# A deformable convolution's offset convolution with its three kernel rows side by side in TensorE's array, and rows and taps that nobody reads left out

## What is computed

```python
om = _conv2d(x, w_off, b_off, STRIDE, PAD)      # 27 channels: off_y, off_x, m for each of 9 taps
off_y, off_x, m = jnp.split(om, 3, axis=1)
mask = jax.nn.sigmoid(m)
py = base_y + kgy + off_y; px = base_x + kgx + off_x
...
sampled = corner(y0, x0, ...) + corner(y0, x0 + 1, ...) + corner(y0 + 1, x0, ...) + corner(y0 + 1, x0 + 1, ...)
out = jnp.einsum('bckhw,ock->bohw', sampled * mask[:, None], weight) + bias
...
x = x + _L0_conv_ref(_gn(x), ...)               # deformable convolution, group norm
x = x + _L1_conv_ref(_gn(x), ...)               # two 3x3 convolutions with ternary weights, batch norms, relu
```

## Time and profile before

| | |
|---|---|
| median of 3 runs | 311.93 us (311.05 to 311.96) |
| profiled execution, its own time | 310.99 us |
| its span | 309.2 us |
| PE matmul busy | 273.2 us (88%) |
| PE weight load busy | 239.6 us (77%) |
| DVE busy | 206.3 us (67%) |
| ACT busy | 177.0 us (57%) |
| POOL busy | 133.6 us (43%) |
| mean granted TensorE clock | 0.978 |

### The profile page before, as it was taken

One profiled execution on the slowest core, in us unless ns is written; L12 is line 12 of the kernel. 1 busy time (PEld: TensorE's weight loads), 2 busy tenths in 40 slices (PEclk: granted clock), 3 DMA queues, 4 the chain that ended last, 5 costly groups with the idle time before them and its releaser, 6 DMA issues.

```text
span 309.2 us, 5008 instructions
## 1 busy us (share of the span) xinstructions
PE 273.2 (88%) x1712; PEld 239.6 (77%) x1712; DVE 206.3 (67%) x426; ACT 177.0 (57%) x334; POOL 133.6 (43%) x189
## 2 busy tenths in 40 slices
PE   2999999799999989998998989998899976999900
PEld 2768787699989889997998889997777755777700
DVE  3798666688998899759878788785253625006184
ACT  2549654688866968977789777882043006321052
POOL 8350376376666858777657966503000000000031
PEclk9999999999999999999999999999999997999985
DMA  7900966844333332333323333200000000000006
GB/s 248 330 3 3 302 202 183 271 126 136 116 114 106 113 88 77 103 107 108 108 64 106 104 103 111 83 0 2 0 0 2 0 0 0 0 2 0 2 36 243
DMA packets 25031, 28.60 MB, mean 93 GB/s; under 512 B 2461, under 2 KB 22541, under 8 KB 25000
## 3 DMA queue, kind: packets, MB, share of 16 engines
q1 hardware_dynamic: 24496, 26.98, 27.2%
q10 hardware_dynamic: 504, 1.24, 1.2%
HBM read 19.87 MB, written 6.78 MB: 86 GB/s over the span
## 4 chain that ended last, share of the span: by engine, by line
PE 71%; DVE 16%; ACT 8%; issue 2%; DMA 1%; ACTq 0%
PE PS L683 23%; PE PS L571 10%; PE PS L534 9%; PE PS L607 5%; PE PS L589 4%; PE PS L608 4%; PE PS L609 4%; PE PS L591 4%; PE PS L590 4%; DVE slo L1179 3%; DVE st L1081 2%; ACT vhi L847 2%; DVE vlo L1186 2%; ACT shi L840 2%; DVE xb L1279 2%
## 5 line engine op out<-in xcount | busy, mean ns | idle before, releaser
L453 POOL TENSOR_TENSOR vt<-rowm,hat 128x1026 f32<-128x1026 f32 x36 | 70.8, 1968 | 37.5 <-PE PS L571 36.8
L1179 DVE TENSOR_TENSOR slo<-PS,shi 114x512 fp32r<-114x512 f32 x72 | 53.6, 751 | 12.8 <-ACT shi L840 12.6
L1186 DVE TENSOR_TENSOR vlo<-PS,vhi 128x576 fp32r<-128x576 f32 (+2 forms) x84 | 50.3, 619 | 13.0 <-ACT vhi L847 13.0
L840 ACT ACTIVATE shi<-PS 114x512 fp32r<-114x512 f32 x72 | 46.3, 652 | 20.0 <-PE PS L571 19.7
L571 PE MATMUL PS<-ident,vt 128*114 128x128 f32 x324 | 47.4, 275 | 1.4 <-DVE nsm L1032 0.7
L847 ACT ACTIVATE vhi<-PS 128x576 fp32r<-128x576 f32 (+2 forms) x84 | 44.0, 546 | 7.4 <-PE PS L591 5.1
L589 PE MATMUL PS<-shi,patch 114*128 114x288 f32 x136 | 43.8, 322 | 1.9 <-DVE omh L1329 1.5
L607 PE MATMUL PS<-vhi,wdhi 128*128 128x256 f32 x144 | 43.0, 299 | 2.1 <-ACT xb L854 2.0
L683 PE MATMUL PS<-xhi,q 128*128 128x512 f32 x144 | 39.6, 422 | 4.2 <-ACT xhi L915 4.2
L473 POOL TENSOR_TENSOR xb<-xb,xs 128x512 f32<-128x512 f32 x3 | 3.7, 1274 | 87.3 <-ACT xb L920 87.3
L591 PE MATMUL PS<-shi,patch 114*128 114x288 f32 x136 | 40.8, 300 | 0.0
(11 more groups left out here) (146 smaller groups left out, 438.4 us busy)
## 6 DMA issues: line engine op xcount, KB each, us to landing
patch<-xt SPq DMA_DIRECT2D x136, 114.0 KB
xt<-xtt SPq DMA_DIRECT2D x4, 1024.0 KB, 7.1
xs<-in_x SPq DMA_DIRECT2D x3, 512.0 KB, 7.4
out<-xb SPq DMA_DIRECT2D x6, 256.0 KB, 2.3
wraw<-in_L_conv_w SPq DMA_DIRECT2D x2, 576.0 KB, 9.0
omr<-omr SPq DMA_DIRECT2D x8, 128.0 KB, 4.2
wd_raw<-in_L_conv_weight ACTq DMA_DIRECT2D x1, 576.0 KB, 6.5
xs<-in_x SPq DMA_DIRECT2D x2, 256.0 KB, 4.2
```

The source lines that it names most:

```text
L453: g.tensor_tensor(vt[:, n % 2, :, :].rearrange("p t (r j) -> p t r j", r=WR), rowm[:, n % 2, :, :].unsqueeze(3).to_broadcast([P, TAPS, WR, ...
L840: a.activation(shi[:, n % 2, lo:hi], S_PS[:, lo:hi], ACT.Copy).then_inc(shi_ok, 1)
L1179: d.tensor_tensor(slo[:, n % 2, lo:hi], S_PS[:, lo:hi], shi[:, n % 2, lo:hi], ALU.subtract).then_inc(slo_ok, 1)
L1186: last = d.tensor_tensor(places(vlo), src, places(vhi), ALU.subtract)
```

## The change

**Offset convolution.** The weights of the three kernel rows stand side by side: `woffT` is now 96 columns (three groups of 32) for each of three horizontal taps, in a `hi` and a `lo` copy. One matmul applies a whole kernel row's column to the centre rows: 6 matmuls on `xhi` (hi and lo weights) and 3 on `xlo` for a half image, 9 instead of 18. The product of `xlo` with the weights' `lo` part is left out. The result, 96 partitions of 512 pixels for each half, goes with the bias through ACT (`tail`) to `omc`, a buffer of 34 rows. Its three groups have still to be shifted by a row against each other and added: PE transposes 32 partitions x 128 pixels at a time (`turn_offsets`, 24 transposes an image, three steps of 8; each step waits until the one before has landed), and DVE adds the three with one reduction a half image (`offsets`). That leaves the offsets at 128 positions (four rows) at once; `replicate` now makes the shifted copies by four DMAs of fewer bytes, `masks` works on 128 partitions x 72 elements instead of 32 x 288, and `largest` likewise.

**Order.** In the head `turn_offsets(b)` is put between the halves of later images; `xlo` of image 1 is made by POOL between its two sums of weights instead of by DVE; SP stores image 0's pixels ahead of `replicate(0)`, and image 1's only after `fetch_patches(0)`; ACT's and DVE's calls are rearranged.

**Left out.** The first pair of an image (rows -1, 0) takes only taps 3 to 8 and the last pair (rows 31, 32) only taps 0 to 5: 192 columns instead of 288. For the ninth chunk the transposes of `vt` are six of 64 columns instead of nine of 128. In the ternary convolutions, taps that would read a border row of zeros do 15 rows instead of 16.

```diff
+        omr = sb("omr", [P, B, K + 1, CH, GRP])
...
-            woffT = sb("woffT", [P, TAPS, P], F32R, own)
+            woffT = sb("woffT", [P, 2, K, STACK], F32R, own)
...
+        def taps_at(n, u):
+            s = 4 * (n % CH) + 2 * u
+            return (K, TAPS) if s == 0 else (0, 2 * K) if s == H else (0, TAPS)
+        def weights_at(m, n, part):
+            v = m.rearrange("k (t p) -> k t p", p=P)
+            t0, t1 = PARTS[part]
+            return v[:, t0:t1, :] if pairs(n) == 2 else v[:, t0:min(t1, 2 * K), 0:P // 2]
...
+        TAP_ORDER = [[K + 1] + [k for k in range(TAPS) if k != K + 1], [k for k in range(TAPS) if k != K + 1] + [K + 1]]
+        def tap_rows(h, k):
+            return (1 if (h, k // K) == (0, 0) else 0), H // 2 - (1 if (h, k // K) == (1, K - 1) else 0)
...
             def replicate(b):
-                sp.wait_ge(off_t, 2 * b + 2)
                 sp.wait_ge(mask_ok, b + 1)
-                for q in range(1, 4):
...
+                for ky in range(1, K):
+                    for src, dst, j in ((0, ky * GRP, 0), (P - ky * GRP, 0, 1)):
+                        n = P - ky * GRP if j == 0 else ky * GRP
+                        sp.dma_start(omr[dst:dst + n, b, K - 1 - ky, j:j + H // 4, :],
+                                     omr[src:src + n, b, K - 1, 0:H // 4, :]).then_inc(rep_in[b], 16)
...
+                if i == 0:
+                    pool.wait_ge(xn_ok, 2)
+                    g.tensor_tensor(inner(xlo, 1), square(plain(1)), inner(xhi, 1), ALU.subtract).then_inc(xlo_second, 1)
...
-                for k in range(TAPS):
-                    r = b % RING * ROWS + h * (H // 2) + k // K
-                    last = t.matmul(OFF_PS[(2 * b + h) % 4], woffT[:, k, :], (xhi, xlo)[part][:, r:r + H // 2, k % K:k % K + W],
-                                    start=(k == 0 and part == 0), stop=(k == TAPS - 1 and part == 1))
+                r = b % RING * ROWS + 1 + h * (H // 2)
+                for kx, lo in PASSES[part]:
+                    last = t.matmul(OFF_PS[(2 * b + h) % 4], woffT[:, lo, kx, :], (xhi, xlo)[part][:, r:r + H // 2, kx:kx + W],
+                                    start=(part, lo, kx) == (0, 0, 0), stop=(part, kx) == (1, K - 1))
...
+            PASSES = [[(kx, lo) for lo in range(2) for kx in range(K)], [(kx, 0) for kx in range(K)]]
+            def turn_offsets(b):
+                if b == 0:
+                    pe.wait_ge(pads, 11)
+                pe.wait_ge(off_tail, 2 * b + 2)
+                for step in range(K):
+                    if step:
+                        pe.wait_ge(off_t, 2 * (K * b + step))
+                    for j in range(4):
+                        for half in range(2):
+                            ky = (step + half) % K
+                            at = slice(ky * GRP, ky * GRP + GRP)
+                            r = 4 * (4 * half + j) + ky
+                            ins = t.transpose(OM_PS[(2 * b + half) % 4][:, j, ky, :], omc[at, b % 2, r * W:r * W + P], ident[at, at])
+                            if j == 3:
+                                ins.then_inc(off_t, 1)
...
-                for tap in range(*PARTS[part]):
-                    last = t.transpose(S_PS[:, tap * P:(tap + 1) * P], vt[:, n % 2, tap, :], ident[:, :])
+                m = P if pairs(n) == 2 else P // 2
+                for tap in range(PARTS[part][0], min(PARTS[part][1], taps_at(n, pairs(n) - 1)[1])):
+                    last = t.transpose(S_PS[:, tap * P:tap * P + m], vt[0:m, n % 2, tap, :], ident[0:m, 0:m])
...
+                a.activation(omc[:, b % 2, (1 + h * (H // 2)) * W:(1 + (h + 1) * (H // 2)) * W], OFF_PS[n % 4],
+                             ACT.Identity, bias=boffc[:, 0:1]).then_inc(off_tail, 1)
...
             def offsets(n):
-                dve.wait_ge(off_tail, n + 1)
...
+                dve.wait_ge(off_t, 2 * K * (n // 2 + 1))
+                d.tensor_reduce(omr[:, n // 2, K - 1, 4 * (n % 2):4 * (n % 2) + 4, 0:OFFC],
+                                OM_PS[n % 4][:, :, :, 0:OFFC].rearrange("p j y c -> p j c y"), AX.X, ALU.add).then_inc(off_sum, 1)
```

More of the change, by code:

```diff
@@ L36 @@
 PATCHES = 4
-OMROWS = 4 * CH
+STACK = 3 * GRP
 VSLOTS = 18
@@ L146, in build @@
         PS = ctx.enter_context(nc.psum_tensor("PS", [P, 2 * B, BIG], F32))
-        OFF_PS = [PS[:, 4 + m, :] for m in range(4)]
+        OFF_PS = [PS[0:STACK, 4 + m, :] for m in range(4)]
+        OM_PS = [PS[:, 4 + m, 0:4 * STACK].rearrange("p (j y c) -> p j y c", j=4, y=K) for m in range(4)]
         T_PS = [PS[:, 2 * m:2 * m + 2, :].rearrange("p a (k c) -> p (a k) c", c=P) for m in range(2)]
@@ L679, in conv_part @@
                 src, ready = ((xhi, xhi_ok), (xlo, xlo_ok))[part] if done is c1_mm else ((xhi, r1hi_ok), (xlo, r1lo_ok))[part]
-                pe.wait_ge(ready, B + b + 1 if done is c1_mm else 2 * b + h + 1 + (h == 0))
-                for k in range(TAPS):
-                    r = b % RING * ROWS + h * (H // 2) + k // K
-                    last = t.matmul(PS[:, 2 * b + h, :], q[:, k, :], src[:, r:r + H // 2, k % K:k % K + W],
-                                    start=(k == 0 and part == 0), stop=(k == TAPS - 1 and part == 1))
+                pe.wait_ge(ready, B + b + 1 - part if done is c1_mm else 2 * b + h + 1 + (h == 0))
+                for i, k in enumerate(TAP_ORDER[part]):
+                    last = t.matmul(tap_out(PS[:, 2 * b + h, :], h, k), q[:, k, :], tap_in(src, b, h, k),
+                                    start=(i == 0 and part == 0), stop=(i == TAPS - 1 and part == 1))
                 if part:
@@ L704, in convolutions @@
                         conv_part(q2, b, m // 2, m % 2, c2_mm)
+            offset_conv(3, 0)
+            turn_offsets(2)
             slot(-2)
-            offset_conv(3, 0)
+            offset_conv(3, 1)
             slot(-1)
-            offset_conv(3, 1)
+            turn_offsets(3)
             for n in range(SPECULATED):
@@ L838, in weights_hi @@
                     act.wait_ge(v_mm, pairs_through(n - 2))
-                lo, hi = (P * tap for tap in PARTS[part])
-                a.activation(shi[:, n % 2, lo:hi], S_PS[:, lo:hi], ACT.Copy).then_inc(shi_ok, 1)
+                a.activation(weights_at(shi[:, n % 2, :], n, part), weights_at(S_PS[:, 0:TAPS * P], n, part),
+                             ACT.Copy).then_inc(shi_ok, 1)
             def sampled_hi(n, u):
@@ L947, in _ @@
             hats(0)
+            tail(4)
+            pixels_hi(2)
             masks(1)
-            pixels_hi(2)
-            tail(4)
+            tail(5)
             hats(1)
             pixels_hi(3)
-            tail(5)
+            tail(6)
             slot(-2)
             masks(2)
-            tail(6)
+            tail(7)
             slot(-1)
-            tail(7)
             masks(3)
@@ L981, in _ @@
                 for q in range(4):
-                    a.activation(omu[q * GRP:(q + 1) * GRP, :, :].rearrange("p (b h) c -> p b (h c)", b=B),
-                                 omr[0:GRP, :, 2:2 + H, :].rearrange("p b h c -> p b (h c)"), ACT.Copy).then_inc(f_om, 1)
+                    for r in range(4):
+                        a.activation(omu[q * GRP:(q + 1) * GRP, :, :].rearrange("p (m r) c -> p m r c", r=4)[:, :, r, :]
+                                     .rearrange("p (b j) c -> p b j c", b=B),
+                                     omr[r * GRP:(r + 1) * GRP, :, K - 1, 0:H // 4, :], ACT.Copy).then_inc(f_om, 1)
                 act.sem_inc(f_z, 2)
```

146 lines of the change are left out of this document (75 added, 71 removed).

## The result

The changed kernel takes **309.74 us** (median of 12 runs, 307.38 to 311.1) against 311.71 us for the kernel before, run beside it (12 runs, 310.79 to 313.92). The ratio is 0.9934, 95% interval 0.9905 to 0.9962: faster by 0.7%, some 2 us, clear of the noise but small. The forecast was 302.3 us with a range of 299.2 to 306.5; 9.6 us were to go and about 2 went in the median, 3.6 in the profiled executions. The profiled one of the change is the fastest of its twelve, so the 3.6 us that its profile accounts for are more than the change gains as a rule.

The account below looks back on a forecast made before the run. PE was taken to bound the head from 20.45 us on, and the chunks. Head 5.3 us plus chunks and convolutions 4.3 us made 9.6 us: 301.4 us for the profiled execution, 302.3 us against the median, range 299.2 to 306.5.

Parts of the forecast that it names:

- The head gives 5.3 us: Head: chunk 0's first `sample` at 51.2 instead of 56.5 us; bounds 2 and 7 us.
- T = 2.4 us: Time of one `turn_offsets` on PE: 24 transposes at 0.07 us plus two waits of 0.35; bounds 2.0 and 3.1.
- The rival in which transposes overlap: Head: neighbouring transposes run two at a time, `turn_offsets` near 1.6 us, chunk 0 2 us sooner, 300.3 us; chance 0.13.
- From 20.45 us on I lay the new order out with these prices: Head, PE alone: fixed prices of 0.249 us a matmul, 0.099 a transpose; PE through at 49.85 against some 54.98.
- The clock rival: Head: small transposes with pauses lower PE's clock until chunk 0, costing 16.7 us, the end at 319; chance 0.04.
- Image 1's `xlo` on POOL ... free: Head: POOL makes it from 18.65 in some 2.5 us, done by 21.4, needed at 24, so it costs nothing.
- The mask is ready at 29.0: Head, image 0: reductions done by 28.1, mask at 29.0, four copies issued at 0.63 us each, POOL starting at 33.5 to 34.
- This store ... issue at 34.7 ... 40 to 41 ... just in time: Head: image 1's store lands at 40 to 41; ACT and DVE finish at 42 to 43.2, PE arrives at 43.4.
- Sum 4.3 us: Chunks and convolutions: samples 1.7 us, transposes 1.1 and 0.2, convolutions 1.3; bounds 2.5 and 5.5.
- it just holds: Chunk 4's patches: fetch starts near 59, issue 3.6 us, landing 2.5 after, against chunk 4's turn near 66.
- signs of being wrong: First `sample` after 54 us, first `sample` released by a DMA, or chunks taking the same 156 us.
- the rival of transposes at full price: Head: each `turn_offsets` takes near 3.1 us; 4 x 0.7 less 0.2 adds 2.6 us, 304.9 us; chance 0.14.

Follow-up runs that it names:

- e3: The changed kernel with 12 matmuls of 512 columns, into an unread bank, where PE waits for the statistics of images 2 and 3: 307.39 us, ratio 0.9832.
- e12: e10 with ninth chunks' six transposes over 128 columns and the replications of images 2 and 3 behind the patches of chunks 8 and 10: 298.84 us.
- e10: e6 with chunk 4's patches ahead of the replications of images 2 and 3, and the first `sample` waiting for two reductions fewer: 302.91 us.
- e6: e3 with e4's DVE order, and image 1's store issued on SP ahead of chunk 0's patches: 302.88 us, ratio 0.9723.
- e8: The changed kernel with only image 1's store issued ahead of chunk 0's patches: 306.55 us, ratio 0.9853.
- e4: The changed kernel with DVE's reductions moved ahead of `pixels_lo(2)` and ahead of `slot(-1)`: 307.39 us, ratio 0.9859.
- e1: The kernel before with only what the change leaves out (192-column samples, six half transposes, convolution taps without border rows): 308.66 us, ratio 0.9882.
- e14: e12 with the change's 64-column transposes back in every ninth chunk: 301.13 us, ratio 0.9668.
- e3t: The changed kernel with 30 transposes of 128x128 in the first gap, instead of e3's 12 matmuls: 306.34 us, ratio 0.9869.
- e13: e12 with everything put back that the change leaves out (samples, transposes and convolutions as large as before): 303.61 us, ratio 0.9746.

## Why the prediction was wrong

**"The head gives 5.3 us": failed.** It gave 1.4. The step that failed is the layout of PE's new order from 20.45 us on with fixed prices and one wait: PE waited 3.34, 1.62, 0.90 and 1.93 us, and behind three of these its clock fell. By its steps:

- *T = 2.4 us*: too high, 1.41 measured. The rival in which transposes overlap was the right one. A weight load of this shape lasts 0.136 us, and with two restarts of some 0.2 us taken off (0.4 for both in the trace) 24 steps take 1.0 us, 0.042 each, so three are under way at once. The Trainium skill ("TensorEngine Tiling (Array Packing)", Key Properties) says that different tiles can load weights and multiply in parallel, and the trace agrees. The columns/1.2 ns of the Trainium skill ("TensorE: Matmul & The Clock Gate", LDWEIGHTS) give 0.107 us a load, an estimate from that page; it was no floor here, with 0.042 a step.
- *"From 20.45 us on I lay the new order out with these prices"*: this step failed first. The sum took the price of 0.099 us a transpose and 0.249 us a matmul as fixed. But image 0 has 18 matmuls where it had 36, and 15 of the 18 saved stood ahead of the point where PE waits for the statistics. These came when they came, so the idle time became 3.34 us and the clock went to 0.50. Square, turn of image 0 and first half of image 1 ended at 27.07 where the forecast's steps, counted from 19.91, give 19.91 + 1.30 + 0.79 + 2.25 = 24.25: 2.8 us late. The clock rival was there at 0.04, but with small transposes as its cause. For this first stretch the cause was the idle time (e3 fills it and the clock stays), and the earlier trace rows had shown what 4.2 us of it do.
- *"Image 1's `xlo` on POOL ... free"*: it was ready in time, but not free. POOL's second sum of weights now runs from 20.33 us, where POOL had been done at 19.99, and DVE's deviation for images 2 and 3 (L1110) lasted until POOL's instruction (L460) ended:

```profile
20.79 0.97 DVE L1110 TENSOR_TENSOR nsm<-nsm 128x2 f32<-128x2 f32 x1
```

```profile
20.33 1.42 POOL L460 TENSOR_TENSOR wscr<-wraw 128x576 f32<-128x576 f32 x1
```

Before, the same instruction took 0.16 us, with POOL idle. In 14 of the 15 kernels with `xlo` on POOL it takes 0.68 to 1.19 us and ends within 0.03 us of POOL's instruction; in e12 the one behind it takes 0.65. In the change this cost little, since PE's matmuls at low clock lasted until 21.9; where the gap is filled, PE waits 0.4 to 0.9 us for it (0.91 in e10). No run puts `xlo` back on DVE.
- *"The mask is ready at 29.0"*: it was at 30.6, by that delay (`turn_offsets` made up 1.0 us of it, but ACT's table load stood behind the copy of the late half image); and the four copies took 0.78 us each to issue, not 0.63. So POOL started at 35.34 and not at 33.5 to 34.
- *"This store ... issue at 34.7 ... 40 to 41 ... just in time"*: issue 37.03, ACT released at 43.40, which is 6.4 us, not 5.8. The term said that this had no slack, and took no loss for it. Nor did it say what the wait would do to the clock. E6 and e8 show the price: 4.7 us from the swap with two other edits in, 3.2 us in the medians and 2.3 us at the first `sample` alone.
- *DVE's order*: the sum did not cost `offsets(2)` and `offsets(3)` behind `pixels_lo(2)`, which waits through ACT for `hats(0)` and so for the copies. That is the 1.62 us at 41.11, and e4 took it away. The last link, reductions behind `weights_lo(1)`, was forecast, with some 1.35 us of waiting (49.85 to 51.2), and came, with 1.93.

With order, store and gap put right the head was as forecast or better: first `sample` at 50.33 in e6 and 48.27 in e12 (51.2 forecast). That e6 comes so close is partly luck. Three `turn_offsets` stand in the chain to 51.2, so with T at 1.41 its own steps give some 48.2; and e6's statistics came late, with the square at 24.01 where the other filled kernels have 22.25 to 23.25. The price of the large matmuls was right, that of the small transposes too high, and the waits were missing.

**"Sum 4.3 us" for chunks and convolutions: 2.2 us seen in the change, 3.4 to 3.7 in e1.** The samples gave 48 x 0.022 = 1.1 us and not 1.7, since 192 columns step by 0.11 to 0.115 and not 0.10. Convolutions 79.21 - 77.61 = 1.6 us (1.3 forecast). The transposes' 1.3 us did not come as summed. Counted from the matmul ahead to the one behind, image 0's ninth chunk went from 0.67 + 0.58 us with nine transposes to 0.66 + 0.46 with six of half size, 0.13 us less where 0.3 were forecast. "24 have half the columns ... I take 0.2" has the wrong sign: by e12 and e14 the half size costs some 0.2 us a chunk in three of the four ninth chunks. Slot 0 lost some 1.4 us more in the change, since it ran at low clock: nine transposes took 1.77 us (56.90 to 58.67) instead of 1.02 before (58.23 to 59.25).

**Patches of chunk 4**: no wait in the change ("it just holds"), but only because chunk 0 came late. When the head was mended they cost 0.77 us, and in e10 2.46 at chunk 5.

**Signs and chances**: two of the three signs of being wrong came, a first `sample` after 54 and chunks that take the same 156 us. Faster was right, by the smaller part of the change; but 0.7% is within the 2% that count as the same, to which the forecast gave 0.01. In the rival of transposes at full price the 0.2 taken off does not follow: by its own steps the chain over DVE ended 1.35 us later than PE's.

## What to carry to other kernels

When an edit takes work from the bounding engine, look at where that engine already waits: work removed ahead of a fixed arrival only makes the wait longer, and on TensorE it can also make the work behind it slower, as the 3.34 us here did. Follow each queue (SP's, DVE's) from its own last release before calling a transfer just in time, and price it with the wait that it makes. A part that measures nothing can be worth its forecast still: here the restructured convolution went from 0 to 8 us by orders and one filled gap, and one swap of two DMA issues took 3.2 us off by itself and 4.7 beside two other edits. Price an instruction from the start of the one ahead to the start of the one behind, and in more than one place.

## What the runs showed of the hardware

- Transposes of 32 rows in neighbouring row groups overlap three deep: 24 in 1.41 us with two restarts in it.
- 30 transposes of 128x128 kept the granted clock at 1.00 through what was a gap of 3.34 us, in one profiled execution. The Trainium skill ("TensorE: Matmul & The Clock Gate", PE-mode transpose) says that these do not count as busy in the same way; the trace of e3t disagrees.
- Idle times lost the clock in some executions and not in others of nearly the same program. Kept: 2.52 us (e4), 1.92 (e3t), and 1.02 with 0.91 behind it (e10). Lost: 2.09 and 1.86 (e3), and 1.06 with 0.91 behind it (e14). In e12 it fell with none over 0.4 us. One program's runs spread by over 4 us with its mean clock (e13).
- A DVE instruction on two columns lasted 0.97 us instead of 0.16 and ended with the POOL instruction that ran beside it (the change; 1.18 us in e10).
- Six transposes with 64 columns took 0.2 us a ninth chunk more than six with 128, from the matmul ahead to the one behind, in three of four chunks (e14, e12). Why is open.
- At the start of a span the profile can give a clock of 1.00 while matmuls step at half pace: three of 512 columns from 10.55 to 11.96 us, 0.47 each, in the kernel before, where later ones take 0.249. In e12 six still stepped by 0.44 at 14.13 to 16.79 us.
